# A three-engine node pipeline at the end of a graph layer: VectorE's additions first, ScalarE's steps moved between, two products in other banks

## The reference, cut to what matters

```python
h = jnp.maximum(_layernorm(x, axis=-1), 0.0)
x = x + _L1_gnn_ref(h, L1_gnn_W1, L1_gnn_W2, L1_gnn_b1, L1_gnn_b2, edge_weight, src, dst)
h = jnp.maximum(_layernorm(x, axis=-1), 0.0)
x = x + _L2_gnn_ref(h, edge_attr_128, ...)      # begins with hn = h @ W_node.T + b_node, then hn[src]

def _L1_gnn_ref(ego, W1, W2, b1, b2, adj_vals, src, dst):
    msgs = ego[src] * adj_vals[:, None]
    lap = jax.ops.segment_sum(msgs, dst, num_segments=N)
    first = (ego + lap) @ W1 + b1
    second = ego * lap @ W2 + b2
    out = jax.nn.leaky_relu(first + second, negative_slope=0.2)
    norm = jnp.sqrt(jnp.sum(out * out, axis=1, keepdims=True))
    return out / jnp.maximum(norm, 1e-12)
```

## Time and profile before

| | |
|---|---|
| median of 3 runs | 4206.68 us (4205.99 to 4207.88) |
| the profiled execution: its time, its span | 4208.87 us, 4207.6 us |
| GpSimd busy | 3014.1 us, 72% of the span, 2943.5 of it in 3116 gathers (L675) |
| VectorE, TensorE, ScalarE busy | 2599.9, 2442.4, 1818.6 us |
| chain that ended last | GpSimd 48%, issue 27%, SyncE's queue 10%, DMA 7%, VectorE 4% |
| granted TensorE clock, mean | 0.775 |
| from layer 1's last gather to layer 2's first (starts) | 2035.20 to 2082.28 us, 47 us |
| TensorE's granted clock in 2042 to 2082 us | 0.62 |

### The profile page before, as it was taken

How to read it: one execution, slowest core, us unless ns; L and a number is a source line. 1 busy time by engine, 2 the same in 40 slices (tenths; PEclk the granted TensorE clock), 3 DMA queues, 4 the chain that set the end, 5 groups by cost and what they waited for, 6 DMA issues and landing times.

```text
span 4207.6 us, 67388 instructions
## 1 busy us (share of the span) xinstructions
PE 2442.4 (58%) x13316; PEld 2042.1 (49%) x13316; DVE 2599.9 (62%) x7231; ACT 1818.6 (43%) x4182; POOL 3014.1 (72%) x3188
## 2 busy tenths in 40 slices
PE   2666666655556666666444444444656666666667
PEld 1455455554445555555444334444545554554556
DVE  4444444443566666667544444344559999999998
ACT  3444444421344444432211111112447887877875
POOL 3777777777677777777477777777747777777764
PEclk8778888776687888877656666666768999889988
DMA  4444444432344344432233333333456222222221
GB/s 132 110 124 118 121 124 116 122 90 66 88 121 124 114 124 118 121 104 68 78 104 107 105 109 104 109 109 109 115 106 119 57 57 57 57 57 58 57 47 31
DMA packets 238975, 405.80 MB, mean 96 GB/s; under 512 B 66706, under 2 KB 137515, under 8 KB 238572
## 3 DMA queue, kind: packets, MB, share of 16 engines
q0 software_dynamic: 99968, 207.33, 20.4%
q10 hardware_dynamic: 78736, 125.09, 10.5%
q1 hardware_dynamic: 59868, 69.07, 5.3%
HBM read 332.15 MB, written 67.78 MB: 95 GB/s over the span
## 4 chain that ended last, share of the span: by engine, by line
POOL 48%; issue 27%; SPq 10%; DMA 7%; DVE 4%; PE 2%; ACT 2%; ACTq 0%; DVEq 0%; POOLq 0%
POOL t_work L675 48%; DMA t_work<-d_T,t_tabG 6%; SPq L636 6%; SPq L702 4%; ACT t_acc L306 0%; PE ps L1914 0%; DVE t_acc L1883 0%; DVE ps L1371 0%; DVE t_x L1946 0%; DVE t_x L986 0%; PE ps L1337 0%; DVE t_halves L837 0%; DVE t_dev L299 0%; DMA t_tabG<-in_wgt 0%; ACTq L224 0%
## 5 line engine op out<-in xcount | busy, mean ns | idle before, releaser
L675 POOL DMA_INDIRECT t_work<-d_T,t_tabG x3116 | 2943.5, 945 | 1072.6 <-issue 922.3
L1337 PE MATMUL ps<-t_work,t_acc 128*128 x2592 | 450.1, 333 | 445.4 <-SPq L734 424.4
L1337 PEld LDWEIGHTS ps<-t_work,t_acc 128*128 128x128 f32 x2592 | 401.2, 238 | 518.7 <-issue 518.2
L1398 DVE TENSOR_TENSOR t_acc<-t_acc,ps 128x128 f32 (+1 forms) x732 | 210.6, 288 | 668.3 <-PE ps L559 342.7
L1387 DVE TENSOR_TENSOR t_hT<-t_work,ps 128x512 f32<-128x512 f32 x244 | 167.3, 686 | 510.8 <-ACT ps L1474 510.6
L1474 ACT COPY ps<-t_acc 128x512 f32 x244 | 140.5, 588 | 788.7 <-SPq L734 781.5
L1337 PE MATMUL ps<-t_hT,t_acc 128*128 128x128 f32 x1296 | 268.6, 392 | 289.6 <-DVE t_acc L1398 285.4
L1337 PEld LDWEIGHTS ps<-t_hT,t_acc 128*128 128x128 f32 x1296 | 252.5, 298 | 307.7 <-DVE t_hT L1387 301.8
L592 ACT ACTIVATE t_acc<-ps,t_bcol 128x1024 f32<-128x1024 f32 x98 | 109.1, 1113 | 660.0 <-DVE ps L605 654.1
L1774 PE MATMUL ps<-t_work,t_hT 128*128 x1960 | 324.0, 315 | 92.7 <-DVE t_acc L1784 77.6
L1337 PE MATMUL ps<-t_work 128*128 x1312 | 235.5, 342 | 243.6 <-SPq L734 221.0
(11 more groups left out here) (189 smaller groups left out, 4413.5 us busy)
## 6 DMA issues: line engine op xcount, KB each, us to landing
d_edge_net<-t_acc ACTq DMA_DIRECT2D x98, 512.0 KB
t_acc<-d_edge_net SPq DMA_DIRECT2D x98, 512.0 KB, 4.0
t_work<-d_T,t_tabG POOLq DMA_INDIRECT x3116
t_acc<-in_edge_attrT ACTq DMA_DIRECT2D x96, 512.0 KB, 4.2
t_acc<-d_T SPq DMA_DIRECT2D x1280, 0.5 KB
t_acc<-d_T SPq DMA_DIRECT2D x640, 0.5 KB
t_work<-d_T SPq DMA_DIRECT2D x640, 0.5 KB
t_acc<-d_T ACTq DMA_DIRECT2D x12, 790.1 KB, 15.6
```

What stands on the lines that cost most here:

```text
L675: pool.indirect_dma_start(out=work[:, at:at + width], out_offset=None, in_=table, in_offset=bass.IndirectOffsetOnAxis(ap=idx[:, g * QUAD + ...
L1337: last = pe.matmul(sums(layer, s, width), masks[s % MASKS][:, k, :], rows_k, start=(k == 0), stop=(k == QUAD - 1))
L1398: dve.tensor_tensor(out=o, in0=o, in1=sums(layer, s, width), op=ALU.add).then_inc(e_acc[layer], 1)
```

## The change

VectorE's step p becomes: the two additions first, then combine, cap_norms, bend, add_normed, measure_rows, bias_rows, centre_rows, then the masks. ScalarE's store_h2 goes behind invert_norms, spread_rows and finish_h2. The products of the groups k = 11 and 12 (LATE) go to banks 0 and 1, which the sums used, and wait for all 244 additions, where they waited for add_normed of k - 2. TensorE's order is as it was. No instruction is added or taken away.

```diff
+        LATE = [k for k in range(len(NODES)) if CLOSED_AT[k] >= PAIRED - 1]
+        assert len(LATE) == 2 and NODE_AT[LATE[0]] >= PAIRED - 1
+
         def z_of(k):
 
-            return ps[:, 6 + k % 2, :]
+            return ps[:, LATE.index(k) if k in LATE else 6 + k % 2, :]
...
             if k == 0:
                 pe.wait_ge(s_pb2, 2 * HALFNET)
-            if k >= 2:
+            if k in LATE:
+                pe.wait_ge(e_acc[1], STEPS)
+            elif k >= 2:
                 pe.wait_ge(s_xs, len(NODES) + k - 1)
...
         def vector_nodes1(p):
 
-            if at_step(p - 5) is not None:
-                bias_rows(at_step(p - 5))
             if at_step(p - 1) is not None:
                 combine(at_step(p - 1))
-
-        def vector_nodes1_behind(p):
-
+            if at_step(p - 3) is not None:
+                cap_norms(at_step(p - 3))
             if at_step(p - 2) is not None:
                 bend(at_step(p - 2))
             if at_step(p - 3) is not None:
-                k = at_step(p - 3)
-                cap_norms(k)
-                add_normed(k)
-                measure_rows(1, k)
-                centre_rows(1, k)
+                add_normed(at_step(p - 3))
+                measure_rows(1, at_step(p - 3))
+            if at_step(p - 5) is not None:
+                bias_rows(at_step(p - 5))
+            if at_step(p - 3) is not None:
+                centre_rows(1, at_step(p - 3))
 
         def scalar_nodes1():
 
             for p in range(NODE_AT[0], NODE_AT[-1] + 6):
-                if at_step(p - 5) is not None:
-                    store_h2(at_step(p - 5))
                 if at_step(p - 3) is not None:
                     k = at_step(p - 3)
                     invert_norms(k)
                     spread_rows(1, k)
                     finish_h2(k)
+                if at_step(p - 5) is not None:
+                    store_h2(at_step(p - 5))
...
             for p in range(-2, NODES_OVER[layer] + 1):
-                if layer == 1:
-                    vector_nodes1(p)
                 if layer == 2:
                     vector_nodes2(p)
...
                 if layer == 1:
-                    vector_nodes1_behind(p)
+                    vector_nodes1(p)
```

## The result

The changed kernel takes 4201.15 us (median of 20 runs, 4198.31 to 4205.08), the kernel before 4206.93 us beside it (20 runs, 4204.9 to 4209.93). The ratio is 0.9985, 95% interval 0.9979 to 0.9991: 5.8 us or 0.14% faster, where 4199.0 us and 0.18% were forecast. It is a gain that can be measured, and it lies within the 0.2% taken as the bound. The profiled execution took 4203.8 us (span 4202.4), mean granted TensorE clock 0.778.

The account below looks back on a forecast made before the run. GpSimd's gathers are not held by the ring, so only the hole between layer 1's last and layer 2's first gather could shrink. The last store comes 7.8 us earlier, taken as 7.7: 4206.7 - 7.7 = 4199.0 us, range 4196.0 to 4203.5.

Parts of the forecast that it names:

- The bound: Layer 1: GpSimd waits only for its own issue; time can come only from the hole between gathers, 2035.20 to 2082.28 us.
- Odd steps: VectorE's steps with masks: 0.60 us wait goes, 0.51 stays, additions cost 0.23; a pair takes 14.8 us, not 15.2.
- Steps 104 to 112: Crowded steps: gains and turn_h2's wait for late bias_rows cancel but for 0.3 us; bounds 2.5 gained, 4 lost.
- The rival with this as its price: Steps 109 to 112: late bias_rows and product_n make steps 13 us, 11.2 us late, 4210.7 us; chance 0.04.
- Ahead of the tail: Step 121 and last sums: centre_rows of k = 8 at 2030.5, additions 2037.0, cap(9) 2038.85; finish_h2(9) ends 3.6 us earlier.
- the gain before the tail doesn't come: Rival: steps 109 to 112 lose what they save; gain 5.6 us, 4201.1; chance 0.19 together with ScalarE's order.
- The banks: Products 11 and 12 in other banks: worth 0, bounds 0 to -1.0 us.
- cap(9) to cap(10): Between the starts of cap_norms of groups 9 and 10: 8.05 us forecast, 12.39 before.
- The tail: After the last sums: combine(12) at 2045.7, 7.3 us earlier; last store issued at 2070.95, 7.8 us earlier.
- the 2050 that was to be a sign of being wrong: Sign in the tail: the prediction is wrong if combine(12) still starts after 2050 us.
- The give-back: In the tail on ScalarE, finish_h2 and the store's issue (0.38 us) precede the next group's squares, returning part of the gain.
- The rival of the high clock: TensorE stays at the high clock in the tail: 2.1 us more gained, 4196.9 us; chance 0.15.

Follow-up runs that it names:

- before_held: The kernel before, with a register instruction max(count, 0) ahead of each wait on a loaded count: 4207.83 us, ratio 1.0003.
- bias_first: The changed kernel with the same register instructions and bias_rows moved back right behind the additions, ahead of combine: 4207.29 us, ratio 1.0000.
- after_held: The changed kernel with a register instruction max(count, 0) ahead of each wait on a loaded count: 4200.2 us, ratio 0.9986.
- the early squares: Changed kernel with register instructions, ScalarE's square_rows moved ahead of spread_rows and finish_h2; run twice on the second chip: ratios 0.9975 and 0.9953.
- clear_late: Changed kernel with register instructions, GpSimd's layer 1 memsets held until the last cap_norms; run twice on the second chip: ratios 0.9964 and 0.9956.
- cap_other_op: Changed kernel with register instructions, the cap written as scalar_tensor_tensor with two tensor inputs; second chip: 5436.98 us, ratio 0.9953.
- cap_square: Changed kernel with register instructions, the cap with two tensor inputs and ScalarE's squares early; second chip: 5443.6 us, ratio 0.9959.

## Why the prediction was right, and where not

- *The bound.* GpSimd waits for its own issue alone up to the last gather, and all of the difference lies in the hole: right.
- *Odd steps.* The idle before centre_rows is gone, the 0.51 us stays: right in the rows. It is right in the size as well: from the additions of step 118 to those of step 120 it is 15.12 us before (2020.80 to 2035.92) and 14.75 after (2021.84 to 2036.59), the 0.37 less that was forecast.
- *Steps 104 to 112.* Gain and loss were to cancel but for 0.3 us gained. They did not: turn_h2 is 5.7 to 6.4 us late, not 3 to 5, and centre_rows of k = 5 (step 113) comes at 1988.36 us in place of 1986.67, 1.7 late; in the other executions it is 1987.16 and 1987.17 against the 1985.96 of `before_held`, 1.2 late. This is within the bounds given (2.5 gained to 4 lost). The late bias_rows is the cause: `bias_first`, with all the rest changed, has it at 1983.20, 4.0 us earlier than `after_held`. The rival with this as its price (11.2 us late, 4210.7) had the direction right and the size too large.
- *Ahead of the tail.* centre_rows of k = 8 was to come at 2030.5 and came at 2032.88, 0.7 later than before. That is the condition of the rival "the gain before the tail doesn't come", and its times fit: additions at 2038.7 (measured 2038.77), centre(9) at 2044.4 (2046.23, and 2044.45 less the hold). The forecast had 2037.0 and 2042.55. cap(9) was 1.88 us late against its 2038.85. Against the last gather the miss looks smaller, 4.27 us where 3.65 was forecast, because in this execution that gather came 1.26 us late; where it didn't, it is 4.63 and 4.59.
- *The banks.* 0 forecast, 0 measured.
- *cap(9) to cap(10).* 8.05 forecast, 8.46 without the hold, 10.23 in the changed kernel. **This is the term that was mis-sized.** The prediction put "cap(9) 2038.85, add_normed(9) 2039.5", 0.65 us between them, from the usual 0.17 us of the cap; it is 2.45 (2040.73 to 2043.18). GpSimd's memsets stand in the very timeline that was read for the gathers, and moving cap(9) 3.5 us earlier put it inside them. The other 0.4 us is likely the 0.66 us that VectorE idles on issue before the last additions, where no mask is in front any more; the forecast put nothing for it here.
- *The tail.* combine(12), forecast for 2045.7 us, started at 2049.92, just inside the 2050 that was to be a sign of being wrong. From cap(10) on, 24.05 us were forecast and 22.94 measured. The mechanism is right: cap(11) and cap(12) wait 2.2 us each for squares that stand behind finish_h2, and against the early squares this order costs 2.4 us. The give-back was put too large. cap(10) to cap(11) is 6.90 us (7.25 forecast) and cap(11) to bias(11) 11.75 (12.5). One reason shows in the rows: the issue of store_h2, counted as 0.38 us ahead of the squares, runs beside finish_h2 (0.38 us from 2055.68, the first of finish_h2's instructions from 2055.67). From bias(11) to the last store it is 4.29 us, exactly as before.
- *The clock.* In the tail the forecast's low clock came true (0.67 and 0.50 in 2048 to 2058 and 2058 to 2075 us). The rival of the high clock isn't wrong as a mechanism: on the second chip, without the hold, TensorE has 1.00 up to product1(12), and the tail is 0.59 us shorter, not 2.1.

The sum: the hole was to shrink by 7.8 us and did by 6.13. Against the forecast there are +0.62 before cap(9), +1.78 for the hold, +0.40 behind it and -1.11 in the tail, 1.7 together. Counted from the span's start, the last store was 2.95 us later than forecast (2073.90 for 2070.95): +1.88 in place of the +0.62, the rest as above. Errors of opposite sign made the forecast better than its parts. The rival "the gain before the tail doesn't come" had its front right, and its time, 4201.1 us, is what was measured; that too is partly luck, for it has neither the hold nor the shorter tail.

## What to carry to other kernels

When an instruction moves in time, look at what the other engines do at its new place, not only at its own queue and its semaphores: a 0.16 us instruction took 1.94 us, most likely because it now fell beside another engine's memsets, and no wait in the trace says so, only its duration. Read a tail in pieces that begin and end on instructions of one chain; pieces of the same order came out equal to 0.02 us across kernels and chips while the medians could not tell 0.2%. But look at TensorE's clock in them before subtracting: 12.39 and 10.75 us are nearly the same order at two clocks, and 12.36 met 12.39 by chance. And choose the point from which a time is counted with care: a gather that came 1.26 us late hid most of the 1.9 us by which cap(9) was late. And in a pipeline that drains, put first on each engine what the next group waits for: the late bias_rows and cap ahead of bend (3.9 us between two caps) and the early squares (2.4 us) are the same move. In the crowded steps ahead, where bias_rows is what TensorE waits for, the late place cost 4.0 us.

## What the runs showed of the hardware

*Which operation is held.* Beside the same row of memsets other operations of VectorE ran at their usual pace: after, combine took 0.69 and 0.68 us at 2039.53 and 2040.13, the additions 0.70 at 2038.77. These read PSUM. In `clear_late` the row stands beside the measuring and centring of group 12, which read and write SBUF alone. There BATCH_NORM_STATS2, with one tensor as source, took 0.28 to 0.30 us each (median 0.28), and centre_rows, a small operation with two tensors, its 0.16:

```profile
2603.41 5.84 POOL L895 MEMSET t_acc<- 128x516 f32 x13 [38.64 <-DVE t_rn L984]
...
2606.39 0.16 DVE L863 SCALAR_TENSOR_TENSOR t_dev<-t_meanvar,t_dev 128x3 f32<-128x3 f32 x1
```

*The same at the gathers.* The cap is also held by the last part of GpSimd's gather instruction. In the twelve traces with the tensor_scalar cap, twelve caps started 0.53 to 0.71 us after a gather did. Each took 0.23 to 0.41 us in place of 0.16 and ended 3 to 11 ns before the gather. In `cap_other_op` and `cap_square`, four caps with two tensor inputs started 0.58 to 0.69 us after a gather, and all took 0.16. First before, where both end at 2013.5, then `cap_square`:

```profile
2012.59 0.94 POOL L675 DMA_INDIRECT t_work<-d_T,t_tabG  x1 [0.30 <-issue]
...
2013.17 0.35 DVE L971 TENSOR_SCALAR t_rn<-t_rn 128x4 f32<-128x4 f32 x1
```

```profile
2467.51 0.94 POOL L681 DMA_INDIRECT t_work<-d_T,t_tabG  x1 [0.30 <-issue]
2468.09 0.16 DVE L982 SCALAR_TENSOR_TENSOR t_rn<-t_rn 128x4 f32<-128x4 f32 x1
```

So at the gathers the edit of the cap shows that the form of the operation decides, twelve of twelve against none of four. That the same holds beside the memsets is not tested.

The Trainium skill (SBUF — State Buffer, Who interferes with whom) says that tensor_scalar can use the second pair of VectorE's ports, which it shares with GpSimd, and that whoever comes first keeps the pair for its whole instruction, the other standing still. The trace agrees as to which operation is held. It doesn't agree as to how long: by that rule cap(9) would have gone on after the memset that was under way (0.54 us), and it stood for 1.4 to 3.1 us, each time to the end of the unbroken row.
